# Transposing the softmax probabilities on TensorE instead of on VectorE and through DRAM

## The reference

```python
x = _layernorm(x + _L0_attn_ref(x, ...), axis=-1)        # attn0
x = _layernorm(x + _L0_xattn_ref(x, ctx_4096, ...), axis=-1)
x = _layernorm(x + _L0_ffn_ref(x, ...), axis=-1)
x = _layernorm(x + _L1_attn_ref(x, ...), axis=-1)        # attn1
x = _layernorm(x + _L1_xattn_ref(x, ctx_4096, ...), axis=-1)   # xattn1
x = _layernorm(x + _L1_ffn_ref(x, ...), axis=-1)
```

```python
q = x @ wq.T; k = x @ wk.T; v = x @ wv.T      # xattn1: k and v from the context, q and k normalised (rms)
s = einsum(q, k) * scale + bias               # attn0: causal mask; attn1: causal mask and ALiBi
p = softmax(s, axis=-1)
o = einsum("bhgnm,bhmd->bhgnd", p, v)         # the sum over keys needs p with the keys on partitions
y = o.reshape(...) @ wo.T
```

## Time and profile before

| | |
|---|---|
| median of three runs | 2399.82 us (2395.9 to 2401.77) |
| profiled execution, its own time | 2401.77 us |
| its span | 2400.0 us |
| PE busy | 2289.1 us |
| DVE, ACT, POOL busy | 1206.0, 780.5, 765.6 us |
| mean granted clock | 0.973 |

### The profile page before, as it was taken

How to read it: one execution, slowest core, us unless ns; L and a number is a source line. 1 busy time by engine, 2 the same in 40 slices (tenths; PEclk the granted TensorE clock), 3 DMA queues, 4 the chain that set the end, 5 groups by cost and what they waited for, 6 DMA issues and landing times. The chain is left out here.

```text
span 2400.0 us, 34599 instructions
## 1 busy us (share of the span) xinstructions
PE 2289.1 (95%) x12210; PEld 1833.6 (76%) x12210; DVE 1206.0 (50%) x2052; ACT 780.5 (33%) x1475; POOL 765.6 (32%) x709
## 2 busy tenths in 40 slices
PE   8999999997999989998999999998899999999989
PEld 6888888875555557886788888887788888888867
DVE  3445544447677633334444444556345454544456
ACT  2233223223677731222322223332232233323321
POOL 4122222203333335444222222211443433333233
PEclk9999999998999999999999999999889999999989
DMA  4222222211000113311221222121121212211120
GB/s 160 80 66 60 76 79 79 57 45 32 18 18 11 64 70 123 105 52 54 81 80 50 67 75 78 56 53 49 59 80 54 57 48 79 67 43 53 53 75 36
DMA packets 120546, 152.43 MB, mean 64 GB/s; under 512 B 16272, under 2 KB 67984, under 8 KB 119952
## 3 DMA queue, kind: packets, MB, share of 16 engines
q1 hardware_dynamic: 120464, 151.33, 21.5%
HBM read 124.02 MB, written 27.26 MB: 63 GB/s over the span
## 5 line engine op out<-in xcount | busy, mean ns | idle before, releaser
L263 PE MATMUL banks<-xTh,wh 128*128 128x512 f32 x1024 | 418.7, 409 | 8.8 <-DVE xTl L1887 7.4
L265 PE MATMUL banks<-xTh,wl 128*128 128x512 f32 x1024 | 404.7, 395 | 0.0
L264 PE MATMUL banks<-xTl,wh 128*128 128x512 f32 x1024 | 403.6, 394 | 0.0
L263 PE MATMUL banks<-woh,oth 128*128 128x512 f32 x768 | 315.6, 411 | 23.3 <-DVE otl L874 16.4
L264 PE MATMUL banks<-wol,oth 128*128 128x512 f32 x768 | 302.5, 394 | 0.0
L961 POOL TENSOR_TENSOR sc_sb<-sc_sb,rs 128x512 f32<-128x512 f32 x96 | 104.3, 1090 | 621.1 <-DVE rs L837 621.1
L265 PE MATMUL banks<-woh,otl 128*128 128x512 f32 x768 | 302.1, 393 | 0.0
L880 DVE TENSOR_TENSOR X<-banks,X 128x512 f32<-128x512 f32 x192 | 132.7, 691 | 324.3 <-PE banks L265 323.9
L693 ACT ACTIVATE q_sb<-banks 128x512 f32<-128x512 f32 x192 | 114.5, 597 | 400.6 <-PE banks L265 400.6
L263 PEld LDWEIGHTS banks<-xTh,wh 128*128 128x128 f32 x1024 | 195.6, 191 | 51.0 <-issue 9.2
L265 PEld LDWEIGHTS banks<-xTh,wl 128*128 128x128 f32 x1024 | 194.9, 190 | 44.0
(11 more groups left out here) (208 smaller groups left out, 4039.9 us busy)
## 6 DMA issues: line engine op xcount, KB each, us to landing
raw<-in_a_in SPq DMA_DIRECT2D x144, 256.0 KB, 2.9
raw<-in_a_out SPq DMA_DIRECT2D x96, 256.0 KB, 2.7
turned<-pq SPq DMA_DIRECT2D x384, 64.0 KB, 2.0
pt<-turned SPq DMA_DIRECT2D x96, 256.0 KB, 2.9
f_q<-in_f_q SPq DMA_DIRECT2D x21, 512.0 KB, 3.9
f_s<-in_f_s SPq DMA_DIRECT2D x21, 512.0 KB, 5.3
X<-in_x SPq DMA_DIRECT2D x1, 2048.0 KB, 10.5
x_craw<-in_ctx SPq DMA_DIRECT2D x8, 256.0 KB, 2.7
```

Of the source, the lines that this page charges most:

```text
L263: nc.tensor.matmul(out, w_hi, x_hi, start=start, stop=False)
L264: nc.tensor.matmul(out, w_hi, x_lo, start=False, stop=False)
L265: return nc.tensor.matmul(out, w_lo, x_hi, start=False, stop=stop)
```

## The change

`TR` leaves the order, and with it the block transpose on DVE, the DRAM tensor `turned`, the buffers `pq` and `pt` and their semaphores. `PT` gets a part on PE: four transposes of 128x128 blocks of `sc_sb` into bank 4, which the attention stages did not use. ACT and DVE then make `pth` and `ptl` from bank 4. Bank 4 has one slot: the transposes of a pair wait until `ptl` of the pair before is made. The blocks are laid out so that PV reads contiguous columns. In the order, `PT0-` moves behind `U_1`; in the last head's order `WO6--` comes first, then `PT0`, `WO7--`, `WS0 WS1`, `PV0`, `PT1`, `WS2 WS3`, `PV1`, `PT2`, and `WO0`. Elsewhere, the output buffer `g_o` of the last block has four slots instead of eight, and the normalisation of tile t waits for the transfer of tile t-4.

```diff
     if rms:
-        ev = events("U_0 PT0- TR2- U_1 WS0- WS1- U_2 PV0- PT1- TR3- WS2- WS3- U_3 WO0- PV1- U_4 KT0 PT2- WO1- U_5 KT1 PV2- WO2- SQ0 "
-                    "U_6 PT3- U_7 WO3- SQ1 PV3- SC0 WO4- SC1 U_8 U_9 WO5- SQ2 TR0 U_10 U_11 TR1 WO6- SQ3 SC2 WO7- SC3")
+        ev = events("U_0 U_1 PT0- WS0- WS1- U_2 PV0- PT1- WS2- WS3- U_3 WO0- PV1- U_4 KT0 PT2- WO1- U_5 KT1 PV2- WO2- SQ0 "
+                    "U_6 PT3- U_7 WO3- SQ1 PV3- SC0 WO4- SC1 U_8 U_9 WO5- SQ2 U_10 U_11 WO6- SQ3 SC2 WO7- SC3")
     else:
-        ev = events("U_0 VT1- PT0- TR2- U_1 WS0- WS1- U_2 PV0- PT1- TR3- WS2- WS3- U_3 WO0- PV1- U_4 PT2- WO1- U_5 PV2- WO2- SC0 "
-                    "PT3- WO3- SC1 U_6 PV3- WO4- U_7 WO5- U_8 TR0 WO6- U_9 TR1 WO7- SC2 U_10 SC3 U_11 VT0")
+        ev = events("U_0 VT1- U_1 PT0- WS0- WS1- U_2 PV0- PT1- WS2- WS3- U_3 WO0- PV1- U_4 PT2- WO1- U_5 PV2- WO2- SC0 "
+                    "PT3- WO3- SC1 U_6 PV3- WO4- U_7 WO5- U_8 WO6- U_9 WO7- SC2 U_10 SC3 U_11 VT0")
     if not project:
-        return events("PT0- TR2- PV0- WO6-- " + ("" if rms else "VT1- ") + "PT1- TR3- WO7-- WS0- WS1- PV1- WS2- WS3- WO0- PT2- WO1- "
+        return events("WO6-- " + ("" if rms else "VT1- ") + "PT0- WO7-- WS0- WS1- PV0- PT1- WS2- WS3- PV1- PT2- WO0- WO1- "
                       "PV2- WO2- PT3- WO3- PV3- WO4- WO5- WO6- WO7-")
...
+            def transpose_probs(i, pair):
+                st.need(pe, "p_ready", 4 * i + pair + 1)
+                st.need(pe, "pt_ready", 4 * i + pair)
+                rows = sc_sb[:, pair, :, :].rearrange("p c s -> p (c s)")
+                for t in range(2):
+                    for c in range(2):
+                        last = nc.tensor.transpose(pb[4][:, (2 * t + c) * P:(2 * t + c + 1) * P],
+                                                   rows[:, (2 * c + t) * P:(2 * c + t + 1) * P], ident[:, :])
+                last.then_inc(A["t_done"], 1)
...
-                        pt_wait(act, st, j, n, 1)
-                        st.need(act, "pv_done", 4 * j + n)
-                        nc.scalar.activation(pth[:, :], pt[:, n % 2, :], ACT.Copy).then_inc(A["pt_hi"], 1)
+                        st.need(act, "t_done", 4 * j + n + 1)
+                        nc.scalar.activation(pth[:, :], pb[4][:, :], ACT.Copy).then_inc(A["pt_hi"], 1)
...
-            def transpose_probs(i, pair):
-
-                st.need(dve, "p_ready", 4 * i + pair + 1)
-                pt_wait(dve, st, i, pair, 0)
-                nc.vector.transpose(pq[:, pair % 2, :].rearrange("p (bk ct i) -> p ct bk i", bk=4, i=32),
-                                    sc_sb[:, pair, :, :].rearrange("p c s -> p (c s)").rearrange(
-                                        "p (ct bk i) -> p ct bk i", bk=4, i=32)).then_inc(A["t_done"], 1)
...
-                        nc.vector.tensor_tensor(ptl[:, :], pt[:, n % 2, :], f32(pth[:, :]),
+                        nc.vector.tensor_tensor(ptl[:, :], pb[4][:, :], f32(pth[:, :]),
                                                 ALU.subtract).then_inc(A["pt_ready"], 1)
...
             def emit(t):
-                dve_normalise(dve, "ffn1", t, xtile(t), g_o[:, t, :])
+                if t >= 4:
+                    dve.wait_ge(gs[f"out{t % 4}"], 16 * (t // 4))
+                dve_normalise(dve, "ffn1", t, xtile(t), g_o[:, t % 4, :])
```

More of the change, by code:

```diff
@@ L309, in program @@
         ld_b = sem("ld_b")
-        pt_in = [sem(f"pt_in{n}") for n in range(2)]
-        pq_out = [sem(f"pq_out{n}") for n in range(2)]
-        turned = nc.dram_tensor("turned", (2, P, 512), F32, kind="Internal").ap()
         xs = {n: sem("x_" + n) for n in (
@@ L321, in program @@
             "in0", "in1", "in2", "in3", "hi", "w", "p1", "ev", "hd", "ch", "exp", "z", "zt", "zhi", "zr", "p2", "res", "xb",
-            "out")}
+            "out0", "out1", "out2", "out3")}
         def stage_end(name):
@@ L418, in spread_rows @@
             return col.rearrange("p (c o) -> p c o", o=1).to_broadcast([P, 8, S])
-        def pt_wait(eng, st, i, pair, more):
-            wait(eng, pt_in[pair % 2], 16 * (16 * st.index + 2 * i + pair // 2 + more))
         def input_quarter(n):
@@ L455, in load_bias @@
                                      ).then_inc(ld_b, 16)
[L457 to L466, removed]
             if st.before:
@@ L490, in sp_attention, with step @@
             load_w(0, 5, 4)
[L492 to L496, removed]
+            def step(i, more):
+                if more:
+                    for c in range(5):
                         if c < 4:
@@ L501, in step @@
                         load_w(i + 1, c, c)
[L502 to L505, removed]
                 for c in range(4):
@@ L511, in step @@
                     load_o(i, c, c)
[L512 to L515, removed]
                 if more:
@@ L519, in step @@
                     load_w(i + 1, 5, 4)
-            step(0, False, True)
+            step(0, True)
             with sp.Fori(1, NKV - 1) as i:
[L523 to L527, removed]
+                step(i, True)
+            step(NKV - 1, False)
         def pe_attention(pe, st):
@@ L601, in probs_v @@
                 st.need(pe, "o_ready", 8 * i + 2 * pair)
-                by_query = [p[:, :].rearrange("p (a c t i) -> p t c a i", a=4, c=2, t=2) for p in (pth, ptl)]
                 for t in range(2):
                     cols = slice(t * G * S, (t + 1) * G * S)
-                    for v_part, p_part in ((vh, 0), (vh, 1), (vl, 0)):
+                    for v_part, p_part in ((vh, pth), (vh, ptl), (vl, pth)):
                         for b in range(2):
                             r = slice(64 * b, 64 * b + 64)
-                            last = nc.tensor.matmul(PVB[b][:, cols], v_part[r, 2 * pair + t, :], by_query[p_part][r, t],
-                                                    start=v_part is vh and p_part == 0, stop=v_part is vl)
+                            last = nc.tensor.matmul(PVB[b][:, cols], v_part[r, 2 * pair + t, :], p_part[r, cols],
+                                                    start=v_part is vh and p_part is pth, stop=v_part is vl)
                 last.then_inc(A["pv_done"], 1)
@@ L638, in run @@
                         transpose_v(j, n)
+                    elif kind == "PT":
+                        transpose_probs(j, n)
                     elif kind == "PV":
@@ L863, in run @@
                         sums(j, n)
-                    elif kind == "TR":
-                        transpose_probs(j, n)
                     elif kind == "PT":
                         st.need(dve, "pt_hi", 4 * j + n + 1)
-                        nc.vector.tensor_tensor(ptl[:, :], pt[:, n % 2, :], f32(pth[:, :]),
+                        nc.vector.tensor_tensor(ptl[:, :], pb[4][:, :], f32(pth[:, :]),
                                                 ALU.subtract).then_inc(A["pt_ready"], 1)
@@ L1681, in sp_ffn1 @@
                 sp.wait_ge(ln_done, 8 * LN_NORMS["ffn1"] + t + 1)
-                sp.dma_start(a["out"][t * P:(t + 1) * P, :], g_o[:, t, :]).then_inc(gs["out"], 16)
-            sp.wait_ge(gs["out"], 16 * NT)
+                sp.dma_start(a["out"][t * P:(t + 1) * P, :], g_o[:, t % 4, :]).then_inc(gs[f"out{t % 4}"], 16)
+            for h in range(4):
+                sp.wait_ge(gs[f"out{h}"], 16 * (NT // 4))
         def pool_split_ffn1(pool, n):
```

4 lines of the change are left out of this document (1 added, 3 removed).

## The result

The changed kernel takes 2420.53 us (median of five runs, 2418.02 to 2422.52), against 2401.77 us for the kernel before beside it: a ratio of 1.0077, with a 95% interval of 1.0064 to 1.0088. It is slower by 18.8 us, where +5 was forecast; the median lies just above the range of 2394 to 2420. The profiled execution took 2417.93 us, with a span of 2416.1, 16.1 us more than before.

What follows compares the result with a forecast made beforehand. TensorE, busy 95%, was taken to bound the kernel. Terms +40 (transposes), -18 (xattn1's hole), -3.5 (`wol` waits) and -13.5 (last heads) gave +5 us: 2405 us against the median 2399.82, range 2394 to 2420.

Steps and rivals of the forecast that it cites:

- The hole in xattn1's heads: TensorE's 2.65 us hole at WO0 in xattn1's heads shrinks to 0.3 us: 18 us back, bounds 10 and 20.
- Wrong would be: Signs against the forecast: transpose starts 200 ns or more apart, xattn1's heads at 78.5 us or above, half clock inside steady heads.
- The transposes, +40 us: 96 groups of four fp32 transposes added on TensorE cost 0.35 to 0.48 us each: +40 us, bounds 34 and 47.
- Rival 4: Each transpose on TensorE costs its full listed 272 ns: 104 in place of 40 us, 2469 us; chance 0.03.
- The small `wol` waits, -3.5 us: In twelve causal heads WO0's wait of about 0.17 us and slower restart go: 0.28 us each, 3.5 us back.
- The last heads, -13.5 us: In the three stages' last heads, the new order gives 15.5 us, less 2 for half clock: 13.5 back, bounds 8 and 19.
- the 2 us taken off: Deduction from the gain in the three last heads, because the new hole at PV1 may bring half clock back.
- `g_o`: Output buffer of four instead of eight tiles: VectorE's work hides the wait for transfers; nothing, or a us or two at the end.
- the transfers: 384 transfers out and 96 in are removed with SP's waits; TensorE nowhere waits for SP's loads once a stage runs: nothing.
- contiguous PV reads: PV's moving operand becomes contiguous: nothing; 5 us if it saved 0.05 us a group.
- Rival 1: Waits are replaced, half of xattn1's hole stays, clock falls behind each new hole: gains 21 us, +19, 2419 us; chance 0.2.
- Rival 2: Holes that go held the clock down: tails give 19 us, xattn1's heads 20; at best -8.5, 2391 us; chance 0.1.

## Why the prediction was wrong

**The step that failed is the term "The hole in xattn1's heads: 18 us back".** Its mechanism held: the hole at WO0 is gone, an undisturbed head takes 77.0 us where 77.4 was forecast, and at full clock the six heads would have gained 7.5 us net of 10 us for transposes. What it left out is the granted clock: I kept half clock inside steady heads only under "Wrong would be", at no price. It took 13.6 us from these heads where it had taken 5.1 before, so the six came out at +1.1 us instead of -7.9. That is 9.0 of the 11.1 us of span that were missed. Over all executions the changed kernel loses 7.6 us more to the clock than the one before. The other line that missed by more than 0.5 us, besides the causal heads below, is the start of attn0 (1.0 us), which no run took apart.

The cause is shown only in part. Shown: in the changed kernel's heads the clock falls in stretches of small matmuls where the profile has no hole; the new transposes are not needed for it (the new order without them loses more of the clock, and causal heads with 16 of them stand at 1.00); and full matmuls added beside the small ones don't reliably stop it. Not shown: what triggers a fall. Four of the falls in kernels with the old order stand right behind a hole, so holes aren't ruled out as one of several triggers. That heads of 78.4 us keep the clock more often is a count over fourteen single executions; the first heads speak against it, and the before kernel with a head of 79.3 us mostly kept its clock too. What it means for the forecast does not: a shorter head of xattn1 was worth nothing in the profiled execution, mean 79.1 us after (474.7 over six) against 78.9 before.

**The transposes, +40 us:** right within its bounds. 0.425 us for a group by doubling, 0.35 to 0.48 forecast; 34.2 us for 96 further groups, the bottom of the 34 to 47, or 36.3 us without the clock's part. Rival 4 is dead. The Trainium skill (TensorE: Matmul & The Clock Gate, Part 4: PE-mode transpose) says that transposes don't count for the clock as matmuls do; no run here shows a loss from that, since 32 transposes a causal head still stand at 1.00, and the kernel with twice the transposes lost no more to the clock over all (68.7 us) than the changed one (71.3). The same page (Why this matters for your kernels) ties a drop of the clock to idle gaps of TensorE; here one drop stands right behind a hole (2.65 us, in the before kernel with three matmuls), but the one from 1.00 to 0.54 above stands in 8 us that the profile has as 8.00 busy.

**The small `wol` waits, -3.5 us:** about half. A causal head grew by 1.53 us, not by 1.66 - 0.28 = 1.38. The old order with transposes on TensorE has 69.01 us, so what was gained there does not come from the order; over the 12 heads that is 1.7 us more than forecast. The cause was incomplete as well. The prediction put the wait down to the block transpose ahead of `wol`; the trace of the kernel before shows a second reason:

```profile
1249.06 1.71 POOL L947 TENSOR_TENSOR wl<-raw,wh 128x512 fp32r<-128x512 f32 x1
1250.16 1.76 DVE L883 TENSOR_TENSOR wol<-raw,woh 128x512 fp32r<-128x512 f32 x2
```

In the twelve causal heads the first `wol` runs beside GpSimd's `wl` and takes 1.15 us instead of 0.68, which is more than the wait of 0.17 us. With the block transpose moved away (`TR3` behind `WS3`) it took 1.78 us and the wait stayed.

**The last heads, -13.5 us:** right in the sum. The new hole of 2.7 us at `PV1` was 2.36, 2.36 and 3.17. From attn0's transposes of `vst` (533.65) to WO0 (546.19) it takes 12.5 us, where 12.6 was forecast and 16.5 stood before. In attn1 it is 13.5 us, with 6.8 us at half clock behind the new hole, which is what the 2 us taken off stood for. The three regions of last heads, transposes counted in, came to -4.3 us, and the terms say -3.9. The new order of the tails alone, in the kernel before, gave 7.3 us of the 13.5; the remaining gain came only together with the transposes on TensorE, and no run takes it apart from the clock in the stages that follow, which lie in the same regions.

**`g_o`, the transfers, contiguous PV reads, nothing each:** nothing in the comparison speaks against it.

**Rival 1** came near the time (2419 us; its gains add up to 21.5 and not 21) by its clause on the clock, but in another place: the hole did not stay, and the clock fell elsewhere. **Rival 2** was right that the last heads get some clock back (23.9 to 17.1 us at half clock), but priced nothing in the steady heads, where it went from 10.2 to 27.3 us.

## What to carry to other kernels

In this kernel TensorE is 95% busy, and a transpose that VectorE and transfers do off the critical path was cheaper than one on TensorE, though that is short; about 0.4 us a group was paid 96 times to save waits that an order alone could save in part. A change that shortens a loop whose body has stretches of small matmuls should be priced at both clock levels, by what the kernel's own disturbed heads cost (up to 5 us each here), before its gain is booked. And a wait in a tail can be mended by what stands between two dependent events: with one output projection moved between `PV0` and `PV1` the longest hole there went from 2.9 to 1.4 us, and that kernel was 0.5% faster than the one before. Last, where a kernel's own time spreads by 17 us, span and granted clock of every execution say more of the clock's part than one profile does.

## What the runs showed of the hardware

- The granted clock fell to 0.5 in a stretch that the profile has as fully busy, with one-column, 64-row and 64-column matmuls (1.00 to 0.54 over 8 us). Three full matmuls more in a head (0.7 us) went with a loss of 77.1 instead of 71.3 us in all, six with 64.2.
- One and the same kernel had a mean granted clock from 0.969 to 0.977 in 52 executions, with spans from 2393.3 to 2410.5 us.
- Four fp32 transposes of 128x128 are listed with 272 ns each and start 108 ns apart; a group costs 0.35 to 0.48 us.
- Two VectorE subtractions took 2.35 us beside a GpSimd subtraction, which itself took 1.68 us, and 1.29 without it. In the kernel before, 12 of 96 such subtractions take over 0.9 us, and these are the twelve that run beside one on GpSimd for over 0.3 us.
